# Attention and mixture-of-experts on one core: shared weights' split, scatters, slot table and Silu's table moved, half the warming, statistics two tiles ahead

## The reference

```python
# attention over features, for each of the 32 sequences (S = 64, d = e = 256)
q = layernorm(x)
scaled = einsum('bsd,bse->bde', q, ctx) / sqrt(256)
attn = softmax(scaled, axis=1)
x = x + einsum('bde,bse->bsd', attn, ctx)
# mixture of experts on z = layernorm(x), 2048 tokens
y, g = split(z @ shared_gw.T); shared = (silu(g) * y) @ shared_dw.T      # HS = 352
scores = sigmoid(z @ gate_w.T); top 2 of 8 by scores + gate_bias, weights normalised
out = sum over the two experts e: w_e * (silu(g_e) * u_e) @ down_w[e].T     # H = 176
x = x + shared + out
```

## Time and profile before

| | before |
|---|---|
| median of 3 runs | 245.96 us (245.94 to 248.5) |
| profiled execution, own time | 246.86 us |
| its span | 245.1 us |
| PE busy | 214.3 us (87%) |
| DVE busy | 164.9 us (67%) |
| ACT busy | 129.8 us (53%) |
| POOL busy | 128.0 us (52%) |
| granted clock, mean | 0.95 |

### The profile page before, as it was taken

How to read it: one execution, slowest core, us unless ns; L and a number is a source line. 1 busy time by engine, 2 the same in 40 slices (tenths; PEclk the granted TensorE clock), 3 DMA queues, 4 the chain that set the end, 5 groups by cost and what they waited for, 6 DMA issues and landing times.

```text
span 245.1 us, 5588 instructions
## 1 busy us (share of the span) xinstructions
PE 214.3 (87%) x1533; PEld 188.5 (77%) x1533; DVE 164.9 (67%) x617; ACT 129.8 (53%) x406; POOL 128.0 (52%) x179
## 2 busy tenths in 40 slices
PE   7676999899999999699469998999999999999900
PEld 7444767677677999599359997999999999899800
DVE  2646586997987597956235598777777776335870
ACT  3645699987875424131134755665666666314700
POOL 4538387687666477787000443444444444503890
PEclk9998899999999999799957999999999999999995
DMA  5898757699111033233211434444444442179541
GB/s 175 276 288 250 248 151 222 209 268 275 63 48 45 27 114 114 94 114 112 71 45 48 134 90 135 132 136 132 138 134 135 133 136 88 67 263 424 173 150 43
DMA packets 25598, 36.15 MB, mean 147 GB/s; under 512 B 5248, under 2 KB 20352, under 8 KB 25184
## 3 DMA queue, kind: packets, MB, share of 16 engines
q1 hardware_dynamic: 22160, 26.22, 35.0%
q0 software_dynamic: 3408, 9.57, 10.7%
HBM read 22.02 MB, written 13.75 MB: 146 GB/s over the span
## 4 chain that ended last, share of the span: by engine, by line
PE 53%; POOL 14%; issue 10%; DVE 6%; ACT 6%; DMA 5%; SPq 3%; POOLq 1%; DVEq 0%; ACTq 0%
POOL slot_rows L453 9%; PE bank L950 9%; PE bank L952 8%; PE bank L951 8%; PE bank L976 4%; PE bank L1093 4%; PE bank L965 3%; DMA sul_raw<-shared_upT 3%; PE bank L1119 3%; PE bank L1043 3%; ACT att L563 2%; PE bank L1131 2%; PE bank L1060 2%; PE bank L1136 2%; PE bank L1135 2%
## 5 line engine op out<-in xcount | busy, mean ns | idle before, releaser
L517 POOL DMA_INDIRECT expert_out<-att,yi x39 | 37.3, 955 | 59.9 <-ACT att L529 59.9
L453 POOL DMA_INDIRECT slot_rows<-z_all,desti x32 | 32.6, 1018 | 8.8 <-issue 8.8
L563 ACT ACTIVATE att<-bank,nb 128x256 f32<-128x256 f32 x64 | 29.3, 473 | 3.2 <-DVE nb L699 3.2
L950 PE MATMUL bank<-uph,xh 128*128 x78 | 29.5, 378 | 1.4 <-DVE xl L898 0.8
L950 PE MATMUL bank<-zTh,suh 128*128 128x256 f32 (+1 forms) x96 | 30.6, 319 | 0.0
L952 PE MATMUL bank<-zTh,sul 128*128 128x256 f32 (+1 forms) x96 | 27.8, 290 | 0.0
L951 PE MATMUL bank<-zTl,suh 128*128 128x256 f32 (+1 forms) x96 | 27.8, 289 | 0.0
L1043 PE MATMUL bank<-sd,s_hm 128*128 128x256 f32 (+1 forms) x96 | 24.4, 393 | 2.1 <-DVE x_all L821 2.0
L951 PE MATMUL bank<-upl,xh 128*128 x78 | 26.0, 333 | 0.0
L952 PE MATMUL bank<-uph,xl 128*128 x78 | 25.8, 331 | 0.0
L898 DVE TENSOR_TENSOR xl<-bank,xh 128x256 fp32r<-128x256 f32 x39 | 16.5, 424 | 12.8 <-ACT xh L529 12.6
(11 more groups left out here) (136 smaller groups left out, 596.3 us busy)
## 6 DMA issues: line engine op xcount, KB each, us to landing
cr<-slot_rows SPq DMA_DIRECT2D x39, 136.0 KB, 2.1
y_all<-expert_out SPq DMA_DIRECT2D x3, 1024.0 KB, 8.7
upl_raw<-up_wT SPq DMA_DIRECT2D x8, 352.0 KB, 3.5
cr<-ctx_kv SPq DMA_DIRECT2D x16, 128.0 KB, 3.5
crT<-ctx_kvT SPq DMA_DIRECT2D x16, 128.0 KB, 2.5
dnl_raw<-down_wT SPq DMA_DIRECT2D x8, 256.0 KB, 3.7
out<-x_all SPq DMA_DIRECT2D x16, 128.0 KB, 1.7
x_all<-x SPq DMA_DIRECT2D x1, 1024.0 KB, 7.8
```

The source lines that it names most:

```text
L453: nc.gpsimd.indirect_dma_start(slot_rows, bass.IndirectOffsetOnAxis(ap=desti[:, k, t:t + 1], axis=0), z_all[:, t, :], None).then_inc(sent, 16)
L517: nc.gpsimd.indirect_dma_start(expert_out, bass.IndirectOffsetOnAxis(ap=yi[:, t:t + 1], axis=0), ys[t % 3], None).then_inc(y_out[t % 3], 16)
L563: last = nc.scalar.activation(att[:, j, m:m + D], ps_s[j][b][:, c * D:(c + 1) * D], ACT.Exp, bias=nb[:, j, n:n + 1], accum_out=rs[:, j, n: ...
L950: mm(o, ah, bh, start=(n == 0), stop=False)
```

## The change

Seven edits. (1) `shared_high` leaves DVE; ACT makes the high part of the shared weights in steps 1 and 2, and POOL's `shared_low` moves to steps 2 and 3, directly behind `values`. (2) Scatters: eleven instead of seven in steps 10 to 16 (two in steps 13 and 15, three in 16), and in step 16 they stand before `deviations`. (3) `slot_table` is cut in three, run in steps 22, 23 and 24. (4) Piece 15 of the shared FFN uses Silu, so that the table load stands before it, and one DVE operation. (5) The last early down product is added to x in the piece before. (6) `FILL` is 2. (7) The statistics of x run ahead (`ahead`): one tile a step up to step 0, two a step in steps 1 to 6, none after, and every step has its own place for them, so that the waits for `nm_done`, `z_done` and `q_done` go. The instructions of (7) have up to three columns instead of two.

```diff
-        stats = sb("stats", [P, 2, 6])
+        stats = sb("stats", [P, NT, 6])
...
-        mv = sb("mv", [P, 2, 2, 2])
...
+        mv = sb("mv", [P, NT + 4, 3, 2])
...
+
+        def ahead(p):
+            return range(p + 3, p + 4) if p <= 0 else range(2 * p + 2, min(2 * p + 4, NT))
+
+
+        def place(k):
+            return [(p + 3, 1 + k - ahead(p)[0]) for p in STEPS if k in ahead(p)][0]
+
         WARM = 10
-        FILL = 4
+        FILL = 2
...
         def sending():
+            halves = [(t, k) for t in range(NT) for k in range(K)]
             at = []
-            for a, b in BATCHES:
-                for t in range(a, b):
-                    for k in range(K):
-                        at.append((max(b + 6, at[-1][0] + 1 if at else 0), t, k))
-            return [(p, t, k) for p, t, k in at if p <= NT], [(t, k) for p, t, k in at if p > NT]
+            for p in range(BATCHES[0][1] + 6, NT + 1):
+                for i in range(3 if p == NT else 2 if p in (NT - 3, NT - 1) else 1):
+                    t, k = halves.pop(0)
+                    assert p >= [b for a, b in BATCHES if a <= t < b][0] + 6
+                    at.append((p, t, k))
+            return at, halves
...
@@ -455,13 +465,8 @@
                     z_all[:, t, :], None).then_inc(sent, 16)
             def deviations(p):
-                j = p % 2
-                n0, n1 = int(not live(p - 1)), 1 + int(live(p + 3))
-
-                if live(p - 3):
-                    pool.wait_ge(z_done, p - 2)
-                if live(p + 1):
-                    pool.wait_ge(q_done, p + 2)
+                j = p + 3
+                n0, n1 = int(not live(p - 1)), 1 + len(ahead(p))
                 pool.wait_ge(var_done, p + 4)
                 nc.gpsimd.tensor_tensor(rstd[:, j, n0:n1], ve[:, j, n0:n1], mhalf[:, n0:n1], ALU.pow).then_inc(c_pool, 1)
...
@@ -488,21 +493,19 @@
             for p in STEPS:
                 if live(p):
                     values(p)
+                if 2 <= p < DC + 2:
+                    shared_low(p - 2)
                 if up_split(p - 1) is not None:
                     expert_low(up_split(p - 1))
-                if not live(p) and (live(p - 1) or live(p + 3)):
-                    deviations(p)
                 for at, t, k in SEND_STEP:
                     if at == p:
                         scatter(t, k)
-                if live(p):
+                if live(p - 1) or len(ahead(p)):
                     deviations(p)
                 if p == -3:
                     prepare()
                 if p == -2:
                     gate_split()
-                if 1 <= p < DC + 1:
-                    shared_low(p - 1)
...
                     if n >= 2:
                         act.wait_ge(shm_done, n - 1)
-                    if n in EARLY:
+                    if n < PAUSE - 1:
                         nc.scalar.activation(s_sg[0:m, n % 2, :], gu(n)[0:m, 0:GN], ACT.Tanh,
                                              scale=0.5).then_inc(ssg_done, 1)
...
             def normalised(p):
-                j = p % 2
                 act.wait_ge(nm_done, p + 4)
                 if live(p + 3):
                     k = p + 3
+                    i, c = place(k)
                     if k >= 2:
                         act.wait_ge(sc_done, B2 * (k - 1))
-                    nc.scalar.activation(q[:, k % 2, :], x_all[:, k, :], ACT.Identity, bias=nm[:, j, 1:2],
-                                         scale=rstd[:, j, 1:2]).then_inc(q_done, 1)
+                    nc.scalar.activation(q[:, k % 2, :], x_all[:, k, :], ACT.Identity, bias=nm[:, i, c:c + 1],
+                                         scale=rstd[:, i, c:c + 1]).then_inc(q_done, 1)
                 if live(p - 1):
-                    k = p - 1
-                    nc.scalar.activation(z_all[:, k, 0:D], x_all[:, k, :], ACT.Identity, bias=nm[:, j, 0:1],
-                                         scale=rstd[:, j, 0:1]).then_inc(z_done, 1)
+                    nc.scalar.activation(z_all[:, p - 1, 0:D], x_all[:, p - 1, :], ACT.Identity, bias=nm[:, p + 3, 0:1],
+                                         scale=rstd[:, p + 3, 0:1]).then_inc(z_done, 1)
...
@@ -601,6 +603,9 @@
                     normalised(p - 1)
                 if p > NT:
                     from_z_bank(p)
+                if 1 <= p < DC + 1:
+                    act.wait_ge(sw_in, 16)
+                    copy(suh[:, p - 1, :], su_raw[:, p - 1, :]).then_inc(sw_high, 1)
                 if up_split(p) is not None:
...
@@ -668,9 +673,8 @@
                 dve.wait_ge(c_dve, mark(ins))
             def stats_1(k):
-                j = k % 2
                 dve.wait_ge(*x_ready(k))
-                return mark(nc.vector.bn_stats(stats[:, j, :], x_all[:, k, :]))
+                return mark(nc.vector.bn_stats(stats[:, k, :], x_all[:, k, :]))
...
             def plus_eps(p, marks):
-                j = p % 2
-                n0, n1 = int(not live(p - 1)), 1 + int(live(p + 3))
+                j = p + 3
+                n0, n1 = int(not live(p - 1)), 1 + len(ahead(p))
                 dve.wait_ge(c_dve, max(marks))
                 if p == -3:
                     dve.wait_ge(vs_done, 2)
-
-                if p >= -1:
-                    dve.wait_ge(nm_done, p + 2)
...
-            def slot_table():
+            def slot_counts():
...
                 link(nc.vector.tensor_reduce(first[:, :], tri[:, :, :], AX.X, ALU.add))
+            def slot_starts():
+
                 nc.vector.tensor_tensor(start[:, 0:E], count[:, :], ebase[:, :], ALU.add).then_inc(count_done, 1)
                 link(nc.vector.tensor_tensor(behind[:, :], ntile[:, :], first[:, :], ALU.add))
...
+
+            def slot_table():
                 link(nc.vector.tensor_tensor(leap[:, :, :], past[0:1, :, :],
...
@@ -807,22 +812,19 @@
                     if n % SC == 0 and n // SC >= 2:
                         dve.wait_ge(sdn_done, GT * (n // SC - 1))
                     g, u = gu(n)[0:m, 0:GN], gu(n)[0:m, GN:2 * GN]
-                    if n in EARLY:
+                    if n < PAUSE - 1:
                         link(nc.vector.scalar_tensor_tensor(s_sg[0:m, n % 2, :], s_sg[0:m, n % 2, :], 1.0, u, ALU.add, ALU.mult))
                         nc.vector.scalar_tensor_tensor(h, s_sg[0:m, n % 2, :], 0.5, g,
                                                        ALU.mult, ALU.mult).then_inc(shm_done, 1)
                     else:
                         nc.vector.tensor_tensor(h, s_sg[0:m, n % 2, :], u, ALU.mult).then_inc(shm_done, 1)
-                for t in DOWNS.get(n - 1, []):
+
+                for t in (DOWNS.get(n - 1, []) if n != PAUSE - 1 else []) + (DOWNS[n] if n == PAUSE - 2 else []):
                     shared_add(t)
             def shared_add(t):
                 dve.wait_ge(sdn_done, t + 1)
                 nc.vector.tensor_tensor(x_all[:, t, :], dn(t), x_all[:, t, :], ALU.add).then_inc(sacc_done, 1)
-
-            def shared_high(piece):
-                dve.wait_ge(sw_in, 16)
-                nc.vector.tensor_copy(suh[:, piece, :], su_raw[:, piece, :]).then_inc(sw_high, 1)
...
             def statistics(p):
                 marks = []
-                if live(p + 3):
-                    n_1 = stats_1(p + 3)
+                n_1 = [stats_1(k) for k in ahead(p)]
                 if live(p - 1):
                     n_2 = stats_2(p - 1)
                 if live(p - 3):
                     z_low(p - 3)
-                if live(p + 3):
-                    marks.append(aggregate(mv[:, p % 2, 1, :], stats[:, (p + 3) % 2, :], n_1))
+                for c, k in enumerate(ahead(p)):
+                    marks.append(aggregate(mv[:, p + 3, 1 + c, :], stats[:, k, :], n_1[c]))
                 if live(p - 1):
-                    marks.append(aggregate(mv[:, p % 2, 0, :], stats2[:, (p - 1) % 2, :], n_2))
+                    marks.append(aggregate(mv[:, p + 3, 0, :], stats2[:, (p - 1) % 2, :], n_2))
                 return marks
...
@@ -879,11 +880,13 @@
                 if after(p):
                     shared_piece(after(p) - 1)
                 routing(p)
-                if 0 <= p < DC:
-                    shared_high(p)
                 if down_split(p - 1) is not None:
                     down_low(down_split(p - 1))
                 if batch(p - 1, 2) == len(BATCHES) - 1:
+                    slot_counts()
+                if batch(p - 2, 2) == len(BATCHES) - 1:
+                    slot_starts()
+                if batch(p - 3, 2) == len(BATCHES) - 1:
                     slot_table()
                     dve.wait_ge(sc_done, B2 * NT)
```

More of the change, by code:

```diff
@@ L85, in xattn_moe_kernel @@
         vT = sb("vT", [P, 2, DC, B2, S])
-        stats = sb("stats", [P, 2, 6])
+        stats = sb("stats", [P, NT, 6])
         stats2 = sb("stats2", [P, 2, 6])
-        mv = sb("mv", [P, 2, 2, 2])
-        ve = sb("ve", [P, 2, 2])
-        rstd = sb("rstd", [P, 2, 2])
-        nm = sb("nm", [P, 2, 2])
-        neg = sb("neg", [P, 2, 2])
```

(11 more changed lines are left out.)

## The result

The changed kernel takes 238.44 us (median of 4 runs, 235.68 to 239.63) against 245.95 us (4 runs of the kernel before beside them): a ratio of **0.9634** with the interval 0.9522 to 0.9746. The run of 239.63 fell in the slower state that some executions of any kernel show, and the ratio leaves it out. The kernel is faster. It lies above the 229 to 237 that the forecast held likeliest, inside the range up to 240, and 5.9 us above the 232.5 forecast: by the medians 7.5 us came of 13.5. Its profiled execution took 238.38 us with a span of 236.7, so the profiled spans differ by 8.4 where the sum said 13.4.

What follows compares the result with a forecast made beforehand. Bounds: waits at the start, ACT from 30 to 50 us, PE from 50 to 75, late scatters. Terms -4.7 - 3.2 - 5.5 = -13.4 from 246.86 gave 233.5, as median 232.5; likeliest 229 to 237, range to 240.

Steps and rivals of the forecast that it cites:

- Part 1: Start: shared weights' split moved off DVE, tile 4's exponentials at 24.6 instead of 28.22; gain 3.6 us.
- Part 2: Attention steps: statistics of two tiles a step cost 1.0 us in steps 4 to 6, win 0.7 from step 7.
- Part 3: PE in steps 10 to 15: halved filler wins 1.7 us, less 0.3 for the doubled scatter in step 13.
- Part 4: POOL's scatters end 3.2 us earlier; late deviations of tile 15 make PE wait 2.1 us at step 18.
- less than 5 us earlier: Sign of a wrong prediction: the experts' first transpose comes less than 5 us earlier than 121.53.
- A: Rival: halved filler brings three more half-clock stretches here and there, 1.6 us each: 237.5; chance 0.09.
- B: Rival: PE stands 2 us or more before the experts' first transpose, half clock returns: 236; chance 0.11.
- Part 5: DVE's slot table in three steps: wins 2.6 us of PE's wait and half clock (bounds 0 and 3.6).
- Part 6: Into the experts: first transpose to fourth expert product takes 7.3 us instead of 12.8, at full clock; gain 5.5.
- E: Rival: the table load is not where it is meant, losing 1.0 us into the experts: 233.5; chance 0.02.
- C: Rival: the start gains only 0.6 us, ACT waiting where DVE waited: 235.5, or 237; chance 0.06.
- D: Rival: slower, half clock in every attention step, 1.6 us a stretch, 24 in all: 256.5; chance 0.03.

Runs made afterwards that it cites:

- e3: The kernel before with only the shared weights' split moved (high part to ACT, low part later on POOL): 244.44 us, ratio 0.9913.
- e5: The changed kernel with one tile's statistics a step instead of two: 237.44 us, ratio 0.9615.
- e2: The changed kernel with four filler products in each step instead of two: 234.96 us, ratio 0.9521.
- e1: The changed kernel with the last deviations (tile 15) before the three scatters of step 16 again: 237.88 us, ratio 0.9641.
- e6: The changed kernel with the slot table in one piece in step 22: 238.09 us, ratio 0.9598.
- e10: e9 with two filler products a step instead of four: 235.37 us, ratio 0.9553.
- e11: The changed kernel with eight filler products where PE waits, before the gate's products of step 18: 234.66 us, ratio 0.9552.
- E0: Not a run but a mark in each profile: PE's first transpose for the experts, at 121.53 us before and 117.47 in the changed kernel.
- e4: The kernel before with only piece 15 on Silu and the last early add one piece earlier: 243.68 us, ratio 0.9815.
- e12: e11 with twelve filler products instead of two in step 0: 233.81 us, ratio 0.9521.
- e9: e7 with eleven instead of sixteen filler products before the experts' first wait: 235.74 us, ratio 0.9589.
- e7: The changed kernel with four fillers a step, one step-16 scatter before the last deviations and two behind, sixteen fillers before the experts: 236.09 us, ratio 0.9546.

## Why the forecast was right, and where it fell short

**Part 1, the split: right.** ACT copies at 15.24 (0.79), tile 2 at 15.94 (16.15 forecast), tile 4 at 24.09 (24.6). e3 alone gives 4.6 at tile 4, 1.0 over the term of 3.6.

**Part 2, two tiles' statistics: near nothing, as forecast, but not by its terms.** +1.0 and -0.7 were forecast. From tile 4 to tile 7 the changed kernel takes 0.46 more than before, but 0.35 of that stays with one tile a step (e5), so it is not the statistics' price. From tile 7 to tile 10 0.3 is won, and e5 does not win it. In sum e5 puts the part at 0.1.

**Part 3, half the warming: mis-sized.** From tile 10 to tile 15 0.65 us came, where -1.7 + 0.3 was forecast (19.5 against 20.1); against four fillers (e2) the gain is 0.9 over all steps. The term took DVE to be late next. But between 50 and 70 us PE stands 1.9 us in three waits, all for POOL's values. Parts 1 to 3 together are -4.6 because part 1's surplus covers it, and because this execution's start was lucky: in the four others with the same start (e1, e6, e10, e11) tile 15 is 2.4 to 3.1 us earlier than before, not 4.6.

**Part 4, the scatters: the step that failed.** "Added wait ... plus 2.1 on PE": the wait came, 2.21 us, in its place, and the last scatter ends at 107.8, 1.1 earlier than forecast (1.27 us each instead of 1.35). But it was priced as time in which PE stands and then goes on at full clock. The clock fell at its end and stayed down 10.2 us, worth 4.5 by e11, so PE's pieces ended late and set E0 at 117.47. That is 4.06 earlier than before, and the clock was below 1 in step 18: by both of its own signs, "less than 5 us earlier" and "PE's clock is below 1 in the steps", the prediction was wrong here, though its total held. The same mechanism stood in rivals A (halved filler, small gaps, price 1.6 a stretch) and B (a stand before the first transpose), and I put it in neither case behind the one stand of over 2 us that I had forecast myself. e5's profile, with the wait and without the fall, lands on the forecast's 44.2.

**Part 5, the slot table: mis-sized.** 1.1 us by e6 instead of 2.6. PE's wait fell from 2.04 to 0.91 and about 1.0 was forecast to remain; the half clock that I added came behind this wait in one profile of four with a wait that long (before; not e3, e4, e6).

**Part 6, into the experts: right to 0.1 us**, with one loss later. The fourth expert product is 7.30 us behind E0 (7.3 forecast, 12.8 before), PE's stand before E0 is nil and the clock 1.00, as forecast. The table load is where it was meant, which answers E, and the first Silu starts 0.02 us after its end (118.29 + 1.28, then 119.59). The Trainium skill, page "ScalarE: Activation LUTs", section "What ACT_TABLE_LOAD costs", puts a drain of 1380 ns beside the load of 1283 ns, 2.66 us in all for a switch. This trace agrees on the load (1.28) and shows no drain, neither behind it nor ahead of it, where ACT's copy ends at 118.28. Later 1.1 us is lost once, between the transposes of slots 32 and 34 (the first slot is 0): PE's weight load waits 0.27 us for rows, PE then stands 0.55 us, and ACT 1.39. e12 has 2.0 us a slot there, but such a break stands at other slots in other executions (slot 30 in e2, 35 in e9). From slot 4 to slot 38 the profiles of before and after take 70.95 and 71.82 us, e12's 70.96. What causes it stays open.

**The rivals.** A and B are what happened, in another place: one long fall, not three short ones. C fell (tile 4 came). D did not come: in the changed kernel's stretches from 12 to 72 us the clock is 1.00, though PE is busy only 17.34 of 20. The chances given add up to 0.91 inside the range up to 240, not to the 8 in 10 that the text names. The Trainium skill, page "TensorE: Matmul & The Clock Gate", section "HAM oscillation — how this bites in real kernels", tells of a fall in every tile's wait. Here waits of 0.3 to 1.4 us in most steps from 12 to 72 us brought none, and single stands of 2.2 and 3.2 us went with one in four of five profiles (after, e2, e6 and e11, not e5).

**The sum.** Put together, e12 does what the sum said: its profiled execution took 233.29 us against the 233.5 worked out, with tile 15 at 69.89 (69.4 forecast) and E0 - t15 43.42 (44.2). The total was right for a PE at full clock, in part because errors cancel (part 1 too small, parts 3 and 5 too large, the scatters too slow), and filler in PE's stands was missing to keep it there. That the changed kernel still fell inside the range owes something to the range's width. It paid about 4.5 us for the fall and 1.1 for the late break.

## What to carry to other kernels

A wait that you forecast on PE has two prices, its length and the clock behind it. Where it is as long as those here (2.2 and 3.2 us), put filler of its own length in it and no more: in e11 it cost nothing, since the useful products came no later, and in e7 filler that ran past the wait cost 1.1 us. Filler spread over all steps costs a little in each (0.9 us in all), and in e2's profile it shortened the fall but did not prevent it; by time e2 and e12 are not told apart (ratio 0.9521 both), but e2's runs spread over 3.5 us and e12's over 1.3. One profile can be a lucky one: read a mark in several kernels that share the code up to it before you book its gain. An early gain counts only if the chain next to last is moved too (e3: 4.3 us at tile 15, 2.0 at the end), so price both limits and see how near they are.

## What the runs showed of the hardware

- After the same stand of 2.21 us the clock fell for 10.2 us in two profiled executions (changed kernel, e6), for 3.4 us in one with more filler before it (e2), and not at all in one (e5). Before the tail a stretch of half clock lasted 3.4, 6.8 or 10.2 us.
- Stands that ended near 12 us were no surer. With four fillers a step, 2.31 us in e9 brought no fall and 2.32 us in e2 brought one of 3.4 us; with two, 2.32 us in the changed kernel brought none, and 2.37 us (e5) and 3.17 us (e11) brought 3.4 us each.
- In the stretch with the fall PE still showed busy 19.79 of 22 us (six products 2.35 instead of 1.46 us): a busy share does not show it, the granted clock does.
- Most scatters of 128 rows follow one another every 1.26 us (0.96 and 0.30 of issue), some 1.3 to 1.8; the mean behind the last deviations is 1.27 us in the changed kernel, where PE's clock fell, and 1.29 in e11, where it did not.
- ACT's table load took 1.28 us, with the copy before it ending 0.01 us ahead and the next Silu starting 0.02 us behind.
